# The down product of a mixture-of-experts kernel in three fp32r terms, its weights split ahead of time in the tile loop

## What is computed

```python
x = x + gnn(layernorm(x), adj, ...)      # attention over the neighbours, then a GRU cell
x = x + ffn(layernorm(x), ...)           # two experts of 16 for each token

# ffn, for each token:
top_probs, top_idx = top_k(softmax(x @ gate_w + gate_b), 2)   # and top_probs is normalised
hidden = silu(x @ w1[e]) * (x @ w2[e])   # w1, w2: 16 x 256 x 512
out    = sum over e of weight[e] * (hidden @ w3[e])           # w3: 16 x 512 x 256
```

## Time and profile before

| | us |
|---|---|
| median of 3 runs (1210.1 to 1216.4) | 1211.3 |
| the profiled execution's own time | 1217.5 |
| its span | 1215.3 |
| TensorE busy | 1132.6 |
| VectorE busy | 1019.6 |
| ScalarE busy | 791.7 |
| GpSimd busy | 422.8 |
| tile loop, first to last tile, from the start of the span | 74 to 736 |
| slot loop | 785 to 1202 |

### The profile page before, as it was taken

How to read it: one execution, slowest core, us unless ns; L and a number is a source line. 1 busy time by engine, 2 the same in 40 slices (tenths; PEclk the granted TensorE clock), 3 DMA queues, 4 the chain that set the end, 5 groups by cost and what they waited for, 6 DMA issues and landing times.

```text
span 1215.3 us, 26029 instructions
## 1 busy us (share of the span) xinstructions
PE 1132.6 (93%) x7573; PEld 1037.7 (85%) x7574; DVE 1019.6 (84%) x2526; ACT 791.7 (65%) x1157; POOL 422.8 (35%) x417
## 2 busy tenths in 40 slices
PE   5969999999999999999999995299999999999995
PEld 4658999999999999999999994188888888888884
DVE  6976899999999999999999976388888888888883
ACT  2576777777777777777777741266666666666662
POOL 3520122222222222222222111446555455565553
PEclk9889999999999999999999998599999999999998
DMA  8242445353434354435444310622534555434330
GB/s 252 35 74 36 77 63 81 64 80 64 78 66 79 66 74 67 77 65 78 68 76 70 62 22 18 170 62 47 149 54 99 151 147 146 98 83 115 93 49 4
DMA packets 64004, 98.99 MB, mean 81 GB/s; under 512 B 11703, under 2 KB 38328, under 8 KB 63906
## 3 DMA queue, kind: packets, MB, share of 16 engines
q0 software_dynamic: 35824, 52.58, 27.7%
q1 hardware_dynamic: 28082, 45.19, 13.4%
HBM read 216.36 MB, written 19.10 MB: 194 GB/s over the span
## 4 chain that ended last, share of the span: by engine, by line
PE 89%; DVE 5%; DMA 3%; issue 1%; ACT 1%; POOL 1%; POOLq 0%; DVEq 0%
PE bank L1389 18%; PE bank L1134 16%; PE bank L1403 11%; PE bank L1235 10%; PE bank L1234 10%; PE bank L1236 10%; PE bank L1260 7%; PE bank L1265 4%; PE bank L1286 1%; PE bank L1155 1%; PE bank L1164 1%; DVE xnv L775 1%; DMA expert_lists<-tok,posi 1%; DMA out<-ysc,cidx 1%; DVE E L804 1%
## 5 line engine op out<-in xcount | busy, mean ns | idle before, releaser
L1234 PE MATMUL bank<-V,pc 128*128 128x258 f32 x1024 | 310.6, 303 | 4.3 <-DVE pc L820 4.3
L1235 PE MATMUL bank<-V,pc 128*128 128x258 f32 x1024 | 291.3, 284 | 0.0
L1236 PE MATMUL bank<-V,pc 128*128 128x258 f32 x1024 | 288.9, 282 | 0.0
L1389 PE MATMUL bank<-wup,xT 128*128 128x512 f32 x948 | 242.0, 404 | 0.9 <-DVE xT L1042 0.9
L525 ACT ACTIVATE pc<-bank 128x512 fp32r<-128x512 f32 x256 | 152.0, 594 | 120.7 <-PE bank L1134 115.5
L1389 PEld LDWEIGHTS bank<-wup,xT 128*128 128x128 f32 x948 | 175.0, 191 | 36.4 <-DVE xT L1042 1.3
L820 DVE TENSOR_TENSOR pc<-bank,pc 128x512 fp32r<-128x512 f32 x256 | 175.5, 686 | 30.3 <-ACT pc L525 28.1
L499 POOL DMA_INDIRECT out<-ysc,cidx x79 | 140.1, 1774 | 172.9 <-DMA out<-ysc,cidx 81.7
L1234 PEld LDWEIGHTS bank<-V,pc 128*128 128x128 f32 x1024 | 193.5, 189 | 5.4 <-DVE pc L820 5.4
L1236 PEld LDWEIGHTS bank<-V,pc 128*128 128x128 f32 x1024 | 195.6, 191 | 0.0
L1235 PEld LDWEIGHTS bank<-V,pc 128*128 128x128 f32 x1024 | 195.4, 191 | 0.0
(11 more groups left out here) (162 smaller groups left out, 1640.9 us busy)
## 6 DMA issues: line engine op xcount, KB each, us to landing
wexp<-in_L_ffn_w SPq DMA_DIRECT2D x243, 512.0 KB, 9.4
adjb<-in_adj POOLq DMA_DIRECT2D x128, 256.0 KB, 4.8
token_rows<-xrow SPq DMA_DIRECT2D x32, 130.0 KB, 5.9
E<-in_x SPq DMA_DIRECT2D x8, 512.0 KB, 9.0
xin<-in_x SPq DMA_DIRECT2D x32, 128.0 KB, 5.5
out<-xin SPq DMA_DIRECT2D x32, 128.0 KB, 4.2
xg<-token_rows,gidx POOLq DMA_INDIRECT x79, 3.5
out<-ysc,cidx POOLq DMA_INDIRECT x79, 3.8
```

The lines of the kernel that those rows point to most:

```text
L1234: mm(acc[:, 0:VW], hi, V[:, j, 0, :], start=j == 0, stop=False)
L1235: mm(acc[:, 0:VW], hi, V[:, j, 1, :], start=False, stop=False)
L1236: ins = mm(acc[:, 0:VW], lo, V[:, j, 0, :], start=False, stop=j == T - 1)
L1389: ins = mm(acc[:, 0:HID], xT[:, r % WR, a, k * P:(k + 1) * P], wup[:, r % 2, n, b, k * HID:(k + 1) * HID], start=(k, a, b) == terms[0], st ...
```

## The change

The down product gets the three-term form of the other products. w3 is split into an fp32r part and a rest in 32 pieces (half an expert's matrix each) during the tile loop: SyncE loads a piece, ScalarE rounds it, VectorE makes the rest, SyncE stores both to a DRAM tensor `w3d`. The slot loop then loads w1, w2 and the two parts of w3, four transfers of 512 KB instead of three, and has WB = 6 buffers. VectorE makes a lo part of `hidT`. The weighting (`ysc`) moves from VectorE to ScalarE, where it stands ahead of the copy of `hidT`; the three small operations on `lanew` move from VectorE to GpSimd, between the gather and the scatter. The table's buffer number becomes the expert's number modulo 6, worked out with a few more small operations.

```diff
-    WB = 8
+    WB = 6
+    HALF = HB * F // 2
...
-        wexp = sb("wexp", [P, WB, 3, KB * HID], F32, fs)
+        wexp = sb("wexp", [P, WB, 2, KB * HID], F32, fs)
+        w3s = sb("w3s", [P, WB, 2, HB * F], F32R, fs)
...
-        hidT = sb("hidT", [P, HB, P], F32, fs)
+        hidT = sb("hidT", [P, 2, HB, P], F32R, fs)
...
+        w3d = nc.dram_tensor("down_weights_split", (NE, 2, P, HB * F), F32, kind="Internal").ap()
+        PIECES = 2 * NE
+        def pieces(i):
+            return [n for n in range(PIECES) if 1 + n * (T - 2) // PIECES == i]
...
+            def store_piece(n):
+                sp.wait_ge(s_w3l, n + 1)
+                for k, part in enumerate((w3h, w3l)):
+                    sp.dma_start(w3d[n // 2, k][:, half(n)], part[:, n % 2, :].bitcast(F32)).then_inc(s_w3s[n % 2], 16)
             for i in range(LAST):
                 body(i)
+                if i == 0:
+                    load_piece(0)
+                    load_piece(1)
+                for n in pieces(i):
+                    store_piece(n)
+                    if n + 2 < PIECES:
+                        load_piece(n + 2)
...
             for k in range(KEPT):
-                for n, wv in enumerate((w1v, w2v, w3v)):
+                for n, wv in enumerate((w1v, w2v)):
                     sp.dma_start(wexp[:, k, n, :], wv[k]).then_inc(s_w0[k], 16)
+                    sp.dma_start(w3s[:, k, n, :].bitcast(F32), w3d[k, n]).then_inc(s_w0[k], 16)
...
+            def lane_weights(s):
+                w, r, e = s % WR, s % GR, esl[:, s:s + 1]
+                pool.wait_ge(s_g[r], s // GR * 16 + 16)
+                if s >= WR:
+                    pool.wait_ge(s_fo, s - (WR - 1))
+                for k in range(2):
+                    nc.gpsimd.tensor_scalar(lanew[:, w, k:k + 1], xg[:, r, F + 2 + k:F + 3 + k], e, xg[:, r, F + k:F + k + 1],
+                                            ALU.is_equal, ALU.mult).then_inc(s_lk, 1)
+                pool.wait_ge(s_lk, 2 * s + 2)
+                nc.gpsimd.tensor_tensor(lanew[:, w, 0:1], lanew[:, w, 0:1], lanew[:, w, 1:2], ALU.add).then_inc(s_lw, 1)
...
             for s in range(SLOTS + 1):
                 if s + AHEAD < SLOTS:
                     gather(s + AHEAD)
+                if s < SLOTS:
+                    lane_weights(s)
                 if s >= 1:
                     scatter(s - 1)
...
+            def piece_hi(n):
+                act.wait_ge(s_w3r[n % 2], n // 2 * 16 + 16)
+                if n >= 2:
+                    act.wait_ge(s_w3s[n % 2], n // 2 * 32)
+                act_copy(w3h[:, n % 2, :], w3r[:, n % 2, :]).then_inc(s_w3h, 1)
...
+                    if c == 6:
+                        for n in pieces(i):
+                            piece_hi(n)
...
+            def weigh(s, v, st):
+                act.wait_ge(s_fy, s + 1)
+                act.wait_ge(s_lw, s + 1)
+                if st is None or st >= WR:
+                    act.wait_ge(s_sc, (s - (WR - 1)) * 16)
+                nc.scalar.activation(ysc[:, v, :], accp[:, 0:F], ACT.Copy, scale=lanew[:, v, 0:1]).then_inc(s_fo, 1)
...
                     split_hi(*ahead, b, 1)
+                if st is None or st >= 1:
+                    weigh(s - 1, (r - 1) % WR, None if st is None else st - 1)
                 act.wait_ge(s_fth, s + 1)
...
+            def piece_lo(n):
+                dve.wait_ge(s_w3h, n + 1)
+                V_.tensor_tensor(w3l[:, n % 2, :], w3r[:, n % 2, :], w3h[:, n % 2, :].bitcast(F32),
+                                 ALU.subtract).then_inc(s_w3l, 1)
...
                     for n in range(2):
                         split_lo(s + 2, (r + 2) % GR, b, n)
-                if st is None or st >= 1:
...
-                    V_.tensor_scalar(ysc[:, v, :], accp[:, 0:F], lanew[:, v, 0:1], None, ALU.mult).then_inc(s_fo, 1)
                 if st is None or st < SLOTS:
...
+                    dve.wait_ge(s_fte, s + 1)
+                    V_.tensor_tensor(hidT[:, 1, :, :].rearrange("p k m -> p (k m)"), tp2[:, :],
+                                     hidT[:, 0, :, :].rearrange("p k m -> p (k m)").bitcast(F32),
+                                     ALU.subtract).then_inc(s_ftl, 1)
...
-                    for k in range(HB):
-                        ins = mm(accp[:, 0:F], hidT[:, k, :],
-                                 wexp[:, one(b1), 2, k * F:(k + 1) * F].rearrange("p o f -> p (o f)"), start=k == 0,
-                                 stop=k == HB - 1)
+                    terms = [(k, i, j) for k in range(HB) for i, j in ((0, 0), (0, 1), (1, 0))]
+                    for k, i, j in terms:
+                        ins = mm(accp[:, 0:F], hidT[:, i, k, :],
+                                 w3s[:, one(b1), j, k * F:(k + 1) * F].rearrange("p o f -> p (o f)"),
+                                 start=(k, i, j) == terms[0], stop=(k, i, j) == terms[-1])
```

More of the change, by code:

```diff
@@ L114, in gnn_moe @@
         wT = sb("wT", [P, 2, 2, KB, G3], F32R, gs)
-        wnat = sb("wnat", [P, 2, 6, F], F32, gs)
+        early = ExitStack()
+        wnat = sb("wnat", [P, 2, 6, F], F32, early)
+        early.close()
+        w3r = sb("w3r", [P, 2, HALF], F32, gs)
+        w3h = sb("w3h", [P, 2, HALF], F32R, gs)
+        w3l = sb("w3l", [P, 2, HALF], F32R, gs)
+        assert 6 * HALF == 12 * F
         wihT = sb("wihT", [P, KB, G3], F32, gs)
@@ L268, in gnn_moe @@
         s_sc = sem("outputs_added")
+        s_lk = sem("lane_choices_done")
         s_lw = sem("lane_weights_done")
@@ L278, in gnn_moe @@
         s_fth = sem("hidden_transposed")
-        s_fte = sem("hiddenT_copied")
+        s_fte = sem("hiddenT_hi_done")
+        s_ftl = sem("hiddenT_lo_done")
+        s_w3r = [sem(f"down_weights_loaded{u}") for u in range(2)]
+        s_w3h = sem("down_weights_hi_done")
+        s_w3l = sem("down_weights_lo_done")
+        s_w3s = [sem(f"down_weights_stored{u}") for u in range(2)]
         s_fy = sem("expert_outputs_done")
@@ L396, in load @@
                     wait_apart(sp, *waits)
-                for n, wv in enumerate((w1v, w2v, w3v)):
+                for n, wv in enumerate((w1v, w2v)):
                     sp.dma_start(wexp[:, one(b), n, :].rearrange("p o f -> p (o f)"),
                                  wv[one(e), :, :].rearrange("o p f -> (o p) f"), cond=new == 1).then_inc(s_w[r], 16)
+                    sp.dma_start(w3s[:, one(b), n, :].rearrange("p o f -> p (o f)").bitcast(F32),
+                                 w3d[one(e), n, :, :].rearrange("o p f -> (o p) f"), cond=new == 1).then_inc(s_w[r], 16)
             slot_iterations(sp, load)
@@ L705, in split_hi @@
                 if n == 0 and st is not None and st < KEPT:
-                    waits.append((s_w0[st], 48))
+                    waits.append((s_w0[st], 64))
                 if n == 0 and st != 0:
-                    waits.append((s_w[r], m * 48 + 48))
+                    waits.append((s_w[r], m * 64 + 64))
                 if st is None or st >= 2:
@@ L743, in slot @@
                     act.wait_ge(s_fy, s)
-                act_copy(hidT[:, :, :].rearrange("p k m -> p (k m)"), tp2[:, :]).then_inc(s_fte, 1)
+                act_copy(hidT[:, 0, :, :].rearrange("p k m -> p (k m)"), tp2[:, :]).then_inc(s_fte, 1)
             slot_iterations(act, slot)
@@ L984, in body @@
                         norm2(i)
+                    if c == 7:
+                        for n in pieces(i):
+                            piece_lo(n)
                     if i == 0:
@@ L1029, in _ @@
             pair_rows(T + 2)
-            SLOT_LINKS = 2
             def split_lo(s, r, b, n):
@@ L1068, in _ @@
             link(V_.tensor_scalar(val[:, NEW:NEW + 1], here, 0.0, late, ALU.is_equal, ALU.mult))
-            link(V_.tensor_copy(sci[:, 0:1], val[:, EXPERT:EXPERT + 1]))
-            link(V_.tensor_single_scalar(sci[:, 1:2], sci[:, 0:1], WB - 1, ALU.bitwise_and))
-            link(V_.tensor_copy(val[:, BUF:BUF + 1], sci[:, 1:2]))
+            link(V_.tensor_copy(val[:, BUF:BUF + 1], val[:, EXPERT:EXPERT + 1]))
+            for lap in range(WB, NE, WB):
+                link(V_.tensor_scalar(near, expert, float(lap), -float(WB), ALU.is_ge, ALU.mult))
+                link(V_.tensor_tensor(val[:, BUF:BUF + 1], val[:, BUF:BUF + 1], near, ALU.add))
+            link(V_.tensor_scalar(val[:, BUF:BUF + 1], val[:, BUF:BUF + 1], float(0), used, ALU.max, ALU.mult))
             V_.tensor_tensor(spread[0:SLOTS, :, :], ident[0:SLOTS, 0:SLOTS].unsqueeze(1).broadcast_to([SLOTS, 3, SLOTS]),
@@ L1089, in _ @@
             tokens_lo(0, 0, 0)
-            slot_base = done[0]
             def slot(s, r, m, st):
-                done[0] = slot_base + s * SLOT_LINKS
                 two_on = st is None or st + 2 < SLOTS
@@ L1396, in slot @@
                     b1 = table(pe, BUF, s - 1)
-                    pe.wait_ge(s_fte, s)
+                    pe.wait_ge(s_ftl, s)
                     if st is None or st >= 2:
```

28 lines of the change are left out of this document (11 added, 17 removed).

## The result

| | us |
|---|---|
| median before (4 runs on this chip, 1210.1 to 1216.4) | 1213.8 |
| median after (4 runs, 1306.6 to 1308.9) | 1308.0 |
| after over before | 1.075, 95% interval 1.072 to 1.079 |
| span of the profiled execution, before and after | 1215.3, 1306.8 |

The account below looks back on a forecast made before the run. TensorE sets both loops now; after the change the slot loop was to run at the scatters' landing rate, with 24.7 us for dearer loads. The span sums to 1237.3, 22 above 1215.3; median 1233, range 1198 to 1256.

Parts of the forecast that it names:

- the down product was to give 0.31: Slot loop, TensorE: down product from 1.73 to 1.42 us, 0.31 saved per slot, 24.5 over 79; slot becomes 4.90.
- The time between the loops: Between tile and slot loops: table operations and eight queued loads instead of six add 3 us, between 0 and 6.
- the wait that moves: Slot loop: weighting also needs `lanew`, queued behind scatter s - 2; scatters may lag 4.5 us, so TensorE runs at their rate.
- GpSimd's three operations at 1.2 us: Slot loop, GpSimd: three one-column operations, bounds 0.7 and 1.7 us, hidden in 1.83 idle after a gather; step 4.71 stays.
- rival 3: Slot loop: VectorE's splits hold GpSimd's lane operations, step 5.4 instead of 4.71, some 32 over the forecast, 1265; chance 0.06.
- the forecast's own sum: Whole span: scatter 13 at 864.2, scatters 13 to 66 take 313.6, 12 steps take 54, 5.5 behind: 1237.3 us.
- the 5.5 behind: End of the kernel: 5.5 us of the span lie behind the start of the last scatter, taken as unchanged.
- The forecast's mechanism: Slot loop: each scatter waits for the previous landing; dearer loads add 1.9 us each, 24.7 over 13, on 288.9.
- VectorE has 1.2 us to spare per tile: Tile loop: a piece adds 0.6 to 0.65 us to VectorE, covered by TensorE in a 20.40 us tile; cost 0.
- Rival 4: Tile loop: the tiles stretch by at most 21 us more; chance 0.02.
- rival 1: Slot loop: scatters keep up and TensorE keeps the loop, all 24.5 us come out less 3; 1190; chance 0.12.
- rival 2: Slot loop: bound by the scatters but loads no dearer, 24.7 us goes; 1208.6, or 1203 with 4.71 steps; chance 0.20.

Follow-up runs that it names:

- lane_ahead: The changed kernel with the lane operations (those on `lanew`) still on GpSimd but made two slots earlier; 1305.1 us, ratio 1.075.
- lane_vector: The changed kernel with the three `lanew` operations back on VectorE, behind its lo part of hidT; 1262.1 us, ratio 1.039.
- two_outputs: lane_vector with scatters going in turn to the output and a second DRAM tensor, their sum left out; 1229.8 us in a single run.
- piece_gpsimd: The changed kernel with the lo part of each w3 piece made on GpSimd in the tile loop; 1319.6 us, ratio 1.086.
- rest_scalar: The changed kernel with a piece's lo part replaced by a second rounding copy on ScalarE, subtraction left out; 1295.0 us in a single run.
- combined: The changed kernel with the `lanew` operations as one VectorE instruction, one piece per tile, its lo part early on GpSimd; 1238.6 us, ratio 1.017.
- before_lane_gpsimd: The kernel before, with only the `lanew` operations moved to GpSimd, between gather and scatter; 1228.3 us, ratio 1.011.
- spread_two: combined with the two parts of w3 loaded one slot after w1 and w2, in bursts of 1 MB; 1283.8 us, ratio 1.054.

## Why the prediction was wrong

**Direction and first steps held.** The slots that nothing held took 4.95, against 4.90: 0.27 less than before, where the down product was to give 0.31. The time between the loops rose by 0.4, inside 0 to 6. Steps of the wait that moves were right in kind: slots at TensorE's pace first, then the weighting waiting for `lanew`, with TensorE's down product behind it.

**Step that failed, 1: GpSimd's three operations at 1.2 us, "after a gather it idles 1.83, which hides them".** Alone they take 0.73 + 0.20, so the price without a hold was even high. Held, they take 2.45 + 0.27 at lane_ahead's slot. Of the rows that I priced from, two were VectorE's own, and GpSimd's stands in 30 of 32 cases beside a VectorE instruction that reads a bank and so has one SBUF input. The stretched scatter issues of the earlier trace rows were the sign to the contrary; I had it as rival 3 and gave it 0.06, on the ground that GpSimd idles. Idle time does not help an instruction that cannot start. Rival 3 was the right mechanism, itself too small: it had 5.4 per step, for 53 steps. Of the 0.97 to 6.37, 0.3 is the hold (most of the pair of splits, not half of it) and most of the rest an idle stretch of 0.6 ahead of the scatter that shows wherever the scatter need not wait for a landing (0.62 to 0.69 in four kernels), hidden by the 1.83 before. And slots took over 6 us from the sixth on, not only from scatter 13.

Against the forecast's own sum: scatter 13 started 34.7 later (10.4 from the stages ahead; 12.5 because slots grew to 6.3 before slot 14; 11.9 because it came 18.0 behind the start of slot 14, not 6.1, GpSimd's queue being behind), scatters 13 to 66 took 341.5 in place of 313.6, and the last 12 steps 60.9 in place of 54. With the 5.5 behind unchanged that is the 69.5 us between 1237.3 and 1306.8.

**The forecast's mechanism was real, but second.** In lane_vector the mean step is 5.86, against a forecast of 5.92 (313.6 by 53), with landings up to 9.2. My sum, with 10.4 more for the tiles, gives 1247.7 for it; the span was 1255.0. That the steps agree so well is partly luck: in two_outputs, where landings bind far less, the mean step is still 5.35 and not 4.90, so the landings gave 0.5 per step, where I had counted on 1.0, and neither what else lengthens these slots nor the lower clock behind the holes was in the sum. In the changed kernel a GpSimd step of 6.4 is 1.7 longer than the 4.71 of a scatter that waits for a landing alone, so most landings fell inside it.

**Step that failed, 2: "VectorE has 1.2 us to spare per tile", cost 0.** Tiles went from 20.41 to 20.77, and with the last tile 13 us were lost. The 1.2 was the window's length less its busy time. In that window 19 pauses of 34 to 36 ns, 0.65 us, stand between a VectorE instruction and the next that reads its result (not 28, as the expectation of piece_gpsimd has it); they are the same in both kernels. The other 0.55 were three waits, two for ScalarE's `pc` and one for GpSimd's `rs`. In the changed kernel's tile the three waits are down to 0.30. So about 0.26 could be used, 0.62 was added and 0.36 came out; rest_scalar shows it from the other side. Rival 4 had this mechanism, with 21 as its ceiling and 0.02 as its chance.

**Not met**: rival 1 (scatters keep up) and rival 2. The load's bytes move 1.7 us longer; how much of that a scatter pays was not measured by itself. Combined, with slots of 4.95 and 2 MB loads, has landings up to 8.9, against 8.2 with 1.5 MB.

**What stays open**: no version here beats the kernel before. The best that has the new down product and leaves nothing out, combined, still has ScalarE waiting 58 us for landings, and TensorE at half its clock behind the holes. A chain of scatters that lands sooner beside the loads might turn it; no run shows that.

## What to carry to other kernels

Before small work goes to GpSimd, look at what VectorE does at that moment: beside instructions with two SBUF inputs the small work costs what is left of their length (here two splits in a row), not its own, and a queue in order passes it on to all behind it. Spare time on an engine is its idle time less the pauses between its own dependent instructions; read the timeline, not the difference in a window. A wait of TensorE can cost more than its own length, by the clock of the work behind it. When a stage has two chains nearly as long as it is, price both against the slot before trusting the one that waits today.

## What the runs showed of the hardware

- The hold goes both ways: VectorE's splits made GpSimd's pair of one-column operations 2.45 instead of 0.73, and GpSimd's 128x512 subtraction (1.29) made VectorE's 128x256 `xrow` 1.40 instead of 0.41, though `xrow` has one wide input, and two one-column ones.
- On GpSimd a subtraction of 128x512 takes 1.29 against VectorE's 0.69, but one-column operations cost 0.36 and 0.20, near VectorE's 0.27 and 0.16.
- A lane operation held by the splits waits for both of them, not for one: in the changed kernel a slot's first one has a median of 2.08, where one split takes 1.22.
- The issue of an indirect DMA is stretched less than an operation is held: in lane_vector scatters beside the splits had a median of 2.20, the others 1.59; in before_lane_gpsimd gathers had 1.54 and 1.01.
- After a stop of TensorE of 3.4 us in combined its granted clock was 0.50 for 3.4 us. In the changed kernel's slot loop, where its longest stop was 2.4, it was 1.00 throughout.
- A queue of conditional transfers has a price of its own: 3.1 us for each burst of two in spread_two.
